# Two edge loops of a graph network on one core: one long scan over all features in place of 32 or 33 short ones

## What is computed

```python
# layer 0, h = relu(layernorm(x))
e = s_src[src] + s_dst[dst]
e = jnp.where(e >= 0, e, LEAKY_SLOPE * e)
m = jax.ops.segment_max(e, dst, num_segments=N)
ex = jnp.exp(e - m[dst])
denom = jax.ops.segment_sum(ex, dst, num_segments=N)
out = jax.ops.segment_sum(h[src] * (ex / denom[dst])[:, None], dst, num_segments=N)
# layer 1, h = relu(layernorm(x + out))
x_hat = h[src] @ A1_w.T + A1_b
y_hat = h[dst] @ A2_w.T + A2_b + rel_emb[etype]
a = jnp.tanh(jax.nn.relu(jnp.sum(x_hat * y_hat, axis=-1) / scale))
nei = jax.ops.segment_sum(a[:, None] * msg, dst, num_segments=N)   # msg: h[src] by the edge type's matrix
h_new = jnp.where((in_deg > 0)[:, None], nei + h[src[last_e]] @ self_loop_weight, 0)
```

## Time and profile before

| | us |
|---|---|
| median of 3 runs | 10522.75 (10521.56 to 10541.11) |
| the profiled execution | 10496.84 |
| its span, first to last instruction | 10495.6 |

### The profile page before, as it was taken

How to read it: one execution, slowest core, us unless ns; L and a number is a source line. 1 busy time by engine, 2 the same in 40 slices (tenths; PEclk the granted TensorE clock), 3 DMA queues, 4 the chain that set the end, 5 groups by cost and what they waited for, 6 DMA issues and landing times.

```text
span 10495.6 us, 26585 instructions
## 1 busy us (share of the span) xinstructions
PE 464.7 (4%) x2021; PEld 223.1 (2%) x2054; DVE 3024.4 (29%) x7102; ACT 416.0 (4%) x1332; POOL 7144.1 (68%) x7050
## 2 busy tenths in 40 slices
PE   0000000000000000000463000000000000000000
PEld 0000000000000000000121000000000000000000
DVE  4421111111111111111463232433334333343332
ACT  0000000000000000000232000000000000000000
POOL 4567777777777777776414776767667676676765
PEclk9999999999999999999786555555555555555555
DMA  5311111111111111111595222222222222222221
GB/s 80 103 40 38 37 37 37 37 37 37 37 37 37 40 39 39 39 38 36 218 377 229 74 56 54 65 62 57 61 59 62 62 57 61 58 63 62 57 61 34
DMA packets 327624, 711.73 MB, mean 68 GB/s; under 512 B 162833, under 2 KB 221662, under 8 KB 306991
## 3 DMA queue, kind: packets, MB, share of 16 engines
q0 software_dynamic: 230048, 250.74, 13.8%
q1 hardware_dynamic: 97405, 459.15, 11.9%
q10 hardware_dynamic: 144, 1.61, 0.0%
HBM read 316.82 MB, written 393.07 MB: 68 GB/s over the span
## 4 chain that ended last, share of the span: by engine, by line
issue 61%; DVE 16%; another core or an unknown queue 13%; DMA 4%; POOL 3%; SPq 1%; ACT 1%; PE 0%; DVEq 0%; POOLq 0%; ACTq 0%
DVE ps L1076 5%; DVE arena L1098 5%; DMA layer_rows<-arena 3%; POOL arena L534 1%; DVE arena L1092 1%; DVE arena L1087 1%; DVE dst_score_of_edge L883 1%; DVE h_nodes L1085 1%; POOL aggregate_nodes L534 1%; POOL dst_score_at_starts L564 1%; DVE aggregate_nodes L1095 1%; SPq L378 0%; DVE dst_score_of_edge L915 0%; SPq L450 0%
## 5 line engine op out<-in xcount | busy, mean ns | idle before, releaser
L534 POOL DMA_INDIRECT arena<-layer_rows,edge_row_index x6448 | 6558.6, 1017 | 2544.2 <-issue 2066.1
L1076 DVE TENSOR_TENSOR_SCAN ps<-ps,last_y_hat,arena 128x62 f32<-128x62 f32 x1664 | 517.3, 344 | 1411.5 <-issue 1055.4
L1098 DVE TENSOR_TENSOR_SCAN arena<-ps,arena,aggregate_nodes 128x62 f32<-128x62 f32 x1664 | 502.9, 337 | 862.6 <-issue 860.5
L966 DVE TENSOR_TENSOR_SCAN arena<-ps,arena 128x62 f32<-128x62 f32 x1716 | 503.5, 335 | 751.6 <-issue 749.6
L950 DVE TENSOR_TENSOR arena<-arena,ps 128x62 f32<-128x62 f32 x52 | 13.9, 268 | 2290.8 <-DMA arena<-layer_rows,edge_row_index 2290.8
L596 POOL DMA_INDIRECT y_hat_at_starts<-aggregate_nodes,start_index x98 | 96.4, 984 | 434.4 <-ACT aggregate_nodes L682 317.1
L1047 DVE COPY arena<-ps 128x512 f32<-128x512 f32 (+1 forms) x294 | 154.2, 574 | 337.8 <-SPq L471 143.4
L776 PE MATMUL ps<-weights_b,arena 128*128 128x512 bf16 x588 | 244.1, 427 | 41.1 <-ACT arena L676 33.7
L775 PE MATMUL ps<-weights_a,arena 128*128 128x512 bf16 (+1 forms) x555 | 236.0, 425 | 194.3 <-ACT arena L676 94.4
L534 POOL DMA_INDIRECT aggregate_nodes<-layer_scans,last_edge_index x196 | 189.6, 967 | 62.0 <-issue 59.1
L796 PE MATMUL ps<-identity,arena 128*32 128x128 f32 x104 | 31.6, 408 | 4463.2 <-issue 3463.1
(11 more groups left out here) (186 smaller groups left out, 1665.5 us busy)
## 6 DMA issues: line engine op xcount, KB each, us to landing
layer_rows<-arena SPq DMA_DIRECT2D x98, 2107.0 KB
arena<-layer_rows,edge_row_index POOLq DMA_INDIRECT x6448
layer_scans<-arena SPq DMA_DIRECT2D x52, 1085.0 KB
y_hat_at_starts<-zeros SPq DMA_DIRECT2D x52, 992.0 KB
arena<-y_hat_at_starts SPq DMA_DIRECT2D x52, 992.0 KB
layer_scans<-arena SPq DMA_DIRECT2D x52, 992.0 KB
even_odd_relation<-arena SPq DMA_DIRECT2D x1, 3224.0 KB
even_odd<-even_odd_relation SPq DMA_DIRECT2D x52, 62.0 KB
```

The costliest lines, as they stand in the source:

```text
L534: pool.indirect_dma_start(tile, None, table, bass.IndirectOffsetOnAxis(ap=index, axis=0)) \
L966: ins = v.tensor_tensor_scan(r0[:, b, :, c], x0[:, 0:K], b0[:, :, c], r0[:, 1 - b, K - 1, c:c + 1], ALU.mult, ALU.add)
L1076: ins = v.tensor_tensor_scan(z1p[:, :, c], contp[b], z1[:, b, :, c], ylast[:, c:c + 1], ALU.mult, ALU.add)
L1098: ins = v.tensor_tensor_scan(r1[:, b, :, c], contp[b], ms[:, :, c], r1[:, 1 - b, K - 1, c:c + 1], ALU.mult, ALU.add)
```

## The change

In both loops the scans of a group become one scan. The operands are laid out feature by feature, each feature with its 62 edges and one extra column of carry: column 0 holds the last value of the group before, with a `keep` of 0 there, so that one flat scan of 33 x 63 = 2079 (layer 0) or 32 x 63 = 2016 elements (layer 1) starts anew at each feature. ACT makes the operands in this layout and turns the result back for the store:

- Layer 0: `x0x` is the exponential repeated for 33 features, `b0t` (now in PSUM) the products by feature, `r0t` the result, and ACT copies it by edge into `r0`, which has one buffer in place of two. ACT's exponential of 124 elements becomes one of 62 and one of 2046.
- Layer 1: ACT writes `keep` for 32 features into `contx` (it was 62 elements in PSUM), copies the carry and `z1` by feature into PSUM (`zp`), where DVE's scan runs in place; the messages go by feature into the same PSUM tile (`msp`), and ACT copies the result `r1t` by edge into `r1`. `z1` and `r1` have one buffer in place of two. SP loads `z1` of the next group after `s_zp`, ahead of the index load.
- The gathers, the stores' contents and POOL's queue are as before.

```diff
 # layer 0, DVE
+                    v.tensor_copy(b0t[:, :, 0], r0t[:, :, K])
...
-                    v.tensor_tensor(b0, g0[:, b, :, 0:D + 1], spread(x0[:, K:2 * K], [P, K, D + 1]), ALU.mult) \
+                    v.tensor_tensor(by_edge(b0t), g0[:, b, :, 0:D + 1], spread(x0b, [P, K, D + 1]), ALU.mult) \
                         .then_inc(s_g0_free, 1)
                     v.wait_ge(s_g0_free, g + 3)
-                    v.wait_ge(s_r0_free, g + 1)
-                    for c in range(D + 1):
-                        ins = v.tensor_tensor_scan(r0[:, b, :, c], x0[:, 0:K], b0[:, :, c],
-                                                   r0[:, 1 - b, K - 1, c:c + 1], ALU.mult, ALU.add)
-                    ins.then_inc(s_r0, 1)
+                    v.tensor_tensor_scan(flat(r0t), flat(x0x), flat(b0t), 0.0, ALU.mult, ALU.add).then_inc(s_scan0, 1)
+                    v.wait_ge(s_scan0, g + 1)
                     v.wait_ge(s_r0, g + 1)
-                    v.wait_ge(s_rx, g + 1)
 # layer 0, ACT
                 act.wait_ge(s_d0, g + 1)
-                act.activation(x0, d0, ACT.Exp).then_inc(s_x0, 1)
+                act.activation(x0b, d0[:, K:2 * K], ACT.Exp)
+                act.activation(x0x[:, :, 1:K + 1], d0[:, 0:K].unsqueeze(1).to_broadcast([P, D + 1, K]), ACT.Exp) \
+                    .then_inc(s_x0, 1)
...
+                act.wait_ge(s_scan0, g + 1)
+                act.activation(r0[:, :, 0:D + 1], by_edge(r0t), ACT.Copy).then_inc(s_r0, 1)
 # layer 1, SP
                 for b in range(2):
+                    sp.wait_ge(s_zp, 2 * it + b + 1)
+                    load1((2 * it + b + 1) * K)
                     sp.wait_ge(s_g1[b], 16 * K * (it + 1))
                     sp.dma_start(idx[:, b, :], row_c[:, bass.ds((2 * it + b + 2) * K, K)]).then_inc(s_idx1[b], 16)
-                    sp.wait_ge(s_z1_used, 2 * it + b + 1)
-                    load1(b, (2 * it + b + 2) * K)
                     store1(b, 2 * it + b, it + 1)
 # layer 1, ACT
+            def y_starts(g):
+                act.activation(contx[:, :, 1:K + 1], cont[:, bass.ds(g * K, K)].unsqueeze(1).to_broadcast([P, D, K]),
+                               ACT.Copy)
+                act.activation(zp[:, :, 0], ylast[:, :], ACT.Copy)
+                act.wait_ge(s_z1, 16 * (g + 1))
+                act.activation(by_edge(zp), z1, ACT.Copy).then_inc(s_zp, 1)
...
+                act.wait_ge(s_scan1, g + 1)
+                if turn is not None:
+                    y_starts(g + 1)
+                act.wait_ge(s_r1_free, g + 1)
+                act.activation(r1, by_edge(r1t), ACT.Copy).then_inc(s_r1, 1)
 # layer 1, DVE
-                    for c in range(D):
-                        ins = v.tensor_tensor_scan(z1p[:, :, c], contp[b], z1[:, b, :, c], ylast[:, c:c + 1],
-                                                   ALU.mult, ALU.add)
-                    ins.then_inc(s_z1_used, 1)
+                    v.tensor_tensor_scan(flat(zp), flat(contx), flat(zp), 0.0, ALU.mult, ALU.add).then_inc(s_z1_used, 1)
...
-                    done(v.tensor_tensor(ms, m1e, m1o, ALU.add))
-                    v.wait_ge(s_r1_free, g + 1)
-                    for c in range(D):
-                        ins = v.tensor_tensor_scan(r1[:, b, :, c], contp[b], ms[:, :, c],
-                                                   r1[:, 1 - b, K - 1, c:c + 1], ALU.mult, ALU.add)
-                    ins.then_inc(s_r1, 1)
+                    done(v.tensor_tensor(by_edge(msp), m1e, by_edge(msp), ALU.add))
+                    v.tensor_tensor_scan(flat(r1t), flat(contx), flat(msp), 0.0, ALU.mult, ALU.add).then_inc(s_scan1, 1)
+                    v.wait_ge(s_scan1, g + 1)
                     v.wait_ge(s_r1, g + 1)
```

More of the change, by code:

```diff
@@ L212, in build @@
         g1 = take([2, K, 2 * W1])
[L213 removed]
+        z1 = take([K, D])
         m1e = take([K, D])
[L215 removed]
+        r1 = take([K, D])
+        r1t = take([D, K + 1])
+        contx = take([D, K + 1])
         lg = take([K])
```

104 lines of the change are left out of this document (56 added, 48 removed).

## The result

The changed kernel takes 10429.4 us (median of 4 runs, 10428.4 to 10432.9) against 10522.5 us (median of 4, 10521.6 to 10541.1) for the kernel before: a ratio of 0.9908, with a 95% interval of 0.9891 to 0.9925. The forecast was 10463 us with a range of 10418 to 10495. The profiled execution took 10430.3 us where that of before took 10496.8, 66.5 us less; the medians lie 93 us apart. The forecast gain was 60 us for both: 6.5 us too small for the profiled execution, and 33 us too small for the medians, which it was made for. Where the other 27 us are, and on what the whole gain rests, the experiments had to tell.

What follows compares the result with a forecast made beforehand. POOL's gathers, at 1.40 us each, were taken to bound both loops. Start +2, layer 0's tail -12, layer 1's loop -20 and its tail -30 sum to -60 us: 10522.75 - 60 = 10463, range 10418 to 10495.

Steps and rivals of the forecast that it cites:

- The bound: Both loops: POOL's gathers bound the time; DVE's own time is on the path only where POOL has nothing to gather.
- DVE's busy time in the loops would be halved: Both loops: 33 and 64 scans become one and two, 7.95 us against 4.5, hardly any of it on the path.
- The pace and the account: Both loops: something behind POOL takes one gather per 1.40 us; POOL, at 1.25, may be some 27 us ahead.
- Start and layer 0's tail: Before layer 0's loop 0.5 to 3.8 us later, taken as +2; after its last gather -10.5 to -13.8, taken as -12.
- Layer 1's loop: Layer 1's gathers: DVE's part after the landing is 10 to 14 us, so POOL's waits of 12 and 25 go; -20.
- leads of 27 and 28.2 us: How far POOL may run ahead of the 1.40 us pace; used for layer 1's loop, saving 18 to 21 us.
- the profile's offset of 26 us from the median: Whole kernel: profiled execution 10496.8 lies 26 us under the median 10522.75; the same -60 us was applied to both.
- Layer 1's tail: After layer 1's last gather: wait of 57.90 us falls to 24.6 to 31.0 as DVE's backlog goes; -30.
- Rival 1: Both loops: DVE's many short instructions hold POOL's pace; without them 1.25 us throughout, about 9570 us; chance 0.08.
- Rival 2: Layer 1's loop: DVE's long instructions stop POOL for their whole length, +551 us, about 11015; chance 0.07.
- Rival 3: Both tails don't shrink, from dear reordering copies or scan operands; only the loop's -20 with +4, 10507 us; chance 0.05.
- a fact of these rows: Layer 0's tail: old scans are slow just after the gathers, store issued 25 us after L959; 7.95 us with POOL idle.

## Why the prediction was right, and where it was not

**The bound.** POOL's gathers bound both loops, and DVE's busy time is hardly on the path: right. 819 us of DVE work went, and 66.5 us of the span. That DVE's busy time in the loops would be halved was too much: it fell by a third (28.3 to 18.1 us in the stretch of layer 0, 158.6 to 104.9 us in that of layer 1); only the scans themselves were halved.

**The pace and the account.** 175 gathers at 1.25, then 1.40, won back after a wait: right in all ten profiles at the slower pace, with DVE or without. The prediction said that the trace doesn't tell what it is. It is not of the kernel alone, since the third chip had none of it. Whether it is of the chip, of its set-up or of the recording stays open; it goes by the gather, not by rows or bytes, and it meets DVE's instructions too. It was a weakness of the argument that both profile and times came from one kind of chip.

**Start and layer 0's tail.** +2 forecast, +1.9 measured; -12 forecast, -12.2 measured. The copy was at the dear end (3.8 us), and the rest of the tail a little cheaper. Not foreseen was the step behind it: POOL's store of the correction waits longer, 2.7 us of the tail's gain. The row of before and the row of after:

```profile
4971.24 1.00 POOL L581 DMA_INDIRECT layer_scans<-carry_fixed,first_segment_end_index  x1 [4.97 <-DVE carry_fixed L1006]
```

```profile
4960.29 1.00 POOL L593 DMA_INDIRECT layer_scans<-carry_fixed,first_segment_end_index  x1 [7.65 <-remote]
```

In after DVE had its part ready at 4957.2, and POOL moved only at 4960.3. The last gather had then ended 29 us before, about the 27 us of the account. But in the run without layer 0's DVE work the same step waited 8.93 us only 16 us after the last gather, so the account alone doesn't explain it, and the cause is open.

**Layer 1's loop.** -20 forecast, -21.5 in the profile: right for the execution that was read (leads of 27 and 28.2 us give 19.8 and 21.0; the 18 of the text needs one of 25). It was mis-sized as a term for the median. And the reason given, a short part of DVE after the landing, leaves out the count: with less busy time than before but 74 instructions in a group POOL still waited 473 us. The waits for DVE cost 21.5, 25.4 and 63.1 us in the three profiles with the short scans (4505.0, 4508.9 and 4546.6 us against 4483.5). The step that failed is the one that took the profile's offset of 26 us from the median as a constant to be added to both kernels. With the change it was gone: the profiled execution took 10430.3 us and the median is 10429.4. The spread of the three timed runs, 20 us, was a sign of it: nothing in POOL's own pace varies like that, and the changed kernel's runs lie within 5 us. The range held 10429.4 because its lower end let the median follow the profile (10496.8 - 68 = 10429), an allowance made without a reason for it; that the time fell inside the range is to that extent luck.

**Layer 1's tail.** -30 forecast, -31.7 measured. The backlog of a group that I read from L1084's start was there, and is gone; the wait of 26.2 us lies in the forecast's 24.6 to 31.0, with the products and sums at the cheap end and the copy at the dear one.

**The rivals.** Rival 1 falls by the run without DVE work: 173.7 us for two groups. But it had half of a truth in it: the number of short instructions does matter, for DVE. At the pace of 1.40 DVE is held beside the gathers, and POOL's pace doesn't change with DVE. Rival 2: POOL's gaps beside long DVE instructions didn't add up to anything; layer 1's loop has its 4483.5 us with the single scans, and 4486.1 with the repeated ones. Rival 3: the tails did shrink.

**Why the short scans in the tail were slow.** The prediction left it at "a fact of these rows". The runs show that it is the count: beside the gathers small writes are held to one per 1.40 us, as POOL's gathers are, and the rows of before show short scans held still for 25 us after the last gather. One long scan pays that once.

## What to carry to other kernels

Where an engine's short instructions have idle time ahead of them that nothing in the profile explains ("issue"), and another engine issues transfers all the while, count instructions, not busy time: here 534 us of work in 1656 instructions were too much, and 683 us in 322 were not. A kernel whose runs spread more than its bounding engine does may have a second limit close behind the first, and the offset between the profiled execution and the median may be just that; it is not to be added to both sides. And a gain that rests on a pace should be timed on more than one chip: here, on a chip with gathers at 1.25 us, the pieces of the long scans cost nothing that could be measured. Where two chips differ that much, compare also how much their traces have recorded.

## What the runs showed of the hardware that I had not expected

- The kernel before takes 10493 to 10541 us where the gathers go at 1.40 us, and 9299 us on a chip where they go at 1.25 us. By the profiles of two changed kernels the loops with the 6324 gathers at these paces make 901 us of 1143 us of difference.
- In the traces with the 1.40 most of the semaphore updates by transfers are missing (19,420 in the changed kernel's), and in those with the 1.25 they are there (120,889 in that of the message scan in pieces).
- The 1.40 us don't depend on the number of rows: with 64 partitions in place of 128 the DMA engines moved 31 GB/s in place of 37 and the pace was the same.
- At that pace DVE starts about one short instruction per gather, 1.40 us, once it has used up a reserve (12 small ones ran at once after a wait of 13 us, and 10 short scans in a row ahead of the held ones).
- ACT reads SBUF with a stride of 252 bytes at 1.87 ns an element (L657, L744) and writes PSUM with the same stride at 0.91 (L723); DVE's products with a strided PSUM side are as fast as contiguous ones, 2.29 us for 2046 elements.
